# Scores and value products in groups of four, with a lag of four half steps, in the latent attention of an eight-core layer

## What is computed

```
q = xn @ Wq
latent = (xn @ Wk + xn @ Wv) @ W_down_kv          # [S, 256]
k_rec, v_rec = latent @ W_up_k, latent @ W_up_v    # 16 heads of 64
scores = (q_h @ k_h.T) * scale
scores = scores * exp(-1e-4 * |i - j|)             # decay over all pairs i, j
attn = softmax(scores)
out = (attn @ v_h) @ Wo
```

## Time and profile before

| | us |
|---|---|
| median of 5 runs | 14,242.7 |
| lowest and highest of them | 14,153.4 and 14,560.6 |
| the profiled execution | 14,151.7 |
| its span, slowest core | 14,150.2 |
| spans of the 8 cores | 14,133.8 to 14,150.2 |

### The profile page before, as it was taken

The page is one execution under the profiler, slowest core; times in us unless marked ns, Lnnn a source line. Parts: engine busy times, 40 slices in busy tenths (PEclk is TensorE's granted clock), DMA queues, the critical chain, the costliest instruction groups (busy, mean ns, idle before and its releaser), DMA issues. The chain is left out here.

```text
span 14150.2 us, 124711 instructions; the slowest of 8 cores (14133.8 to 14150.2 us)
## 1 busy us (share of the span) xinstructions
PE 12668.3 (90%) x47470; PEld 4550.2 (32%) x48256; DVE 2484.7 (18%) x3494; ACT 3977.7 (28%) x3948; POOL 140.9 (1%) x165
## 2 busy tenths in 40 slices
PE   1789989989998995899999999997799999999998
PEld 0321111111111111344444444443344444444443
DVE  2211121121112112211111111111211111111111
ACT  4135545545554551111111111111111111111111
POOL 0000000000000000000000000000000000000000
PEclk9965555555555556999999999998899999999999
DMA  2000000000000003222222222222322222222222
GB/s 61 33 2 6 5 11 5 5 11 5 5 6 10 6 5 127 54 36 36 42 36 40 38 36 36 36 36 70 73 36 36 36 36 36 39 40 38 41 36 48
DMA packets 201402, 459.02 MB, mean 32 GB/s; under 512 B 12025, under 2 KB 17145, under 8 KB 200066
## 3 DMA queue, kind: packets, MB, share of 16 engines
q0 software_dynamic: 157184, 320.38, 13.3%
q1 hardware_dynamic: 43650, 130.61, 2.8%
HBM read 708.15 MB, written 50.59 MB: 54 GB/s over the span
## 5 line engine op out<-in xcount | busy, mean ns | idle before, releaser
L987 PE MATMUL yp<-wd_sb,a1s 128*128 128x512 bf16 x18060 | 3980.7, 379 | 215.8 <-ACT a1s L1006 196.6
L971 PE MATMUL h1p<-xnTh,wu_sb 128*128 128x512 bf16 x18066 | 3986.5, 379 | 66.9 <-DMA wu_sb<-wut 47.8
L1006 ACT ACTIVATE a1s<-h1p,bu_sb 128x1024 bf16<-128x1024 f32 x1152 | 1282.3, 1113 | 6827.0 <-PE h1p L971 6827.0
L987 PEld LDWEIGHTS yp<-wd_sb,a1s 128*128 128x128 bf16 x18432 | 1793.4, 98 | 2403.2 <-issue 262.2
L971 PEld LDWEIGHTS h1p<-xnTh,wu_sb 128*128 128x128 bf16 x18432 | 1804.4, 98 | 2227.4 <-issue 55.9
L1030 DVE SCALAR_TENSOR_TENSOR comb<-yp,wgt,comb 128x1024 f32<-128x1024 f32 x1024 | 1314.5, 1284 | 5998.0 <-PE yp L987 5998.0
L707 ACT ACTIVATE expT<-scp,consts 128x1024 bf16<-128x1024 f32 x1792 | 1982.4, 1113 | 1343.3 <-PE scp L626 1340.5
L647 PE MATMUL pvp<-expT,vrec 128*65 128x512 bf16 x3584 | 1897.4, 632 | 179.8 <-ACT expT L707 179.8
L626 PE MATMUL scp<-qstg,krecTP 64*128 64x512 bf16 x2304 | 1164.7, 619 | 8.4 <-DVE qstg L757 8.4
L766 DVE TENSOR_TENSOR sTbB<-scp,decayR 128x512 bf16<-128x512 f32 x512 | 328.5, 686 | 3754.0 <-PE scp L626 3753.9
L626 PE MATMUL scp<-qstg,krecTM 64*128 64x512 bf16 x1792 | 923.8, 617 | 0.0
(11 more groups left out here) (105 smaller groups left out, 2122.2 us busy)
## 6 DMA issues: line engine op xcount, KB each, us to landing
wu_sb<-wut POOLq DMA_DIRECT2D x64, 2048.0 KB, 15.8
wd_sb<-wdt POOLq DMA_DIRECT2D x64, 2048.0 KB, 15.5
xst<-x SPq DMA_DIRECT2D x64, 512.0 KB
bcsb<-rr_dram SPq DMA_DIRECT2D x128, 128.0 KB
attn_sp<-ast SPq DMA_DIRECT2D x32, 512.0 KB
att<-attn_sp SPq DMA_DIRECT2D x32, 512.0 KB
wu_sb<-swut POOLq DMA_DIRECT2D x8, 2048.0 KB, 15.7
wd_sb<-swdt POOLq DMA_DIRECT2D x8, 2048.0 KB, 15.4
```

The costliest lines, as they stand in the source:

```text
L971: last = te.matmul(h1p[(tc * NFT + ft) % 2][:, no:no + nw], wu_sb[:, kc * FCB + ft * 128:kc * FCB + (ft + 1) * 128], xnTh[:, kc * TH + tc ...
L987: last = te.matmul(yp[tt % 2][:, no:no + nw], a1s[:, kc * TC + tti * 128:kc * TC + (tti + 1) * 128], wd_sb[:, kc * D + no:kc * D + no + nw ...
L1006: s_s4.inc(sc.activation(a1s[:, ft * TC:(ft + 1) * TC], h1p[(tc * NFT + ft) % 2][:, :], AF.Gelu, bias=bu_sb[:, (e % 2) * 32 + fc * NFT + f ...
```

## The change

Four things change in the second block of each group, and one in the allocation.

1. TensorE's order. Scores and values are issued in blocks of two half steps: scores of `hk0` and `hk0` + 1 (four matmuls), then the values of two half steps taken from a list `pending` that keeps the last `LAG` = 4 half steps back, also over the end of a job; the list is drained at the end of a group. All waits of a block (one for ScalarE, for the later of the exps that free the score tiles and those that feed the values; for `qstg` at a job's start; for the evacuation) stand at its head.
2. `expT` has six slots instead of three, and the diagonal tiles use the same slots: `sTbB` is gone, and so is `rln` (Ln writes into `rr_sb`, and Exp works in place).
3. ScalarE computes Ln and Exp of job J - 1 (`emit_lnrr`) behind the first `LSL` = 4 exps of job J. The first job of a group has two Identity activations of one element there instead, to keep the count. `exp_done` and `rr_done` give the new counts.
4. VectorE's diagonal products wait for the value matmuls of six half steps before, instead of for the end of the previous job.
5. `scp` and `pvp` are allocated once for all groups, and `krp` and `vrp` are parts of `scp[0]` and `scp[1]`; the first block of a group waits for the counts of the group before.

```diff
-                expT = sb2("expT", [128, 3 * 1024], BF16)
-                sTbB = sb2("sTbB", [128, 2048], BF16)
+                expT = sb2("expT", [128, 6 * 1024], BF16)
...
+                LAG = min(4, NHK)
+                LSL = min(4, NHK)
+                SB = SQ2 * JPG + 2
+
+                def exp_done(J, hk):
+                    gj, pj = divmod(J, JPG)
+                    return gj * SB + SQ2 * pj + hk + 1 + (2 if hk >= LSL else 0)
+
+                def rr_done(J):
+                    gj, pj = divmod(J, JPG)
+                    if pj == JPG - 1:
+                        return (gj + 1) * SB
+                    return gj * SB + SQ2 * (pj + 1) + LSL + 2
...
+                scp = [stps2.enter_context(nc.psum_tensor(f"scp{i}", [128, 1024], F32)) for i in range(3)]
+                pvp = [stps2.enter_context(nc.psum_tensor(f"pvp{i}", [128, 512], F32)) for i in range(2)]
...
+                        krp = [scp[0][:, i * 512:(i + 1) * 512] for i in range(2)]
+                        vrp = [scp[1][:, i * 512:i * 512 + 256] for i in range(2)]
...
-                            for pj in range(JPG):
-                                for hk in range(NHK):
-                                    emit_sc(pj, hk)
-                                    if hk >= 1:
-                                        emit_pv(pj, hk - 1)
-                                emit_pv(pj, NHK - 1)
+                            pending = []
+                            for pj in range(JPG):
+                                J, lam, qc = jinfo(pj)
+                                for b in range(NHK // 2):
+                                    hk0 = 2 * b
+                                    pops = []
+                                    pending.append((J, hk0))
+                                    pending.append((J, hk0 + 1))
+                                    while len(pending) > LAG:
+                                        pops.append(pending.pop(0))
+                                    scw = 0
+                                    lh1 = NHK * J + hk0 + 1
+                                    if lh1 >= 3:
+                                        Jp, hkp = divmod(lh1 - 3, NHK)
+                                        scw = exp_done(Jp, hkp)
+                                    for (Jv, hkv) in pops:
+                                        scw = max(scw, exp_done(Jv, hkv))
+                                    if scw:
+                                        te.wait_ge(s_s2m.sem, scw)
+                                    if hk0 == 0:
+                                        te.wait_ge(s_v2m.sem, vseg(J) + 2)
+                                    for (Jv, hkv) in pops:
+                                        if hkv == 0 and Jv >= 2:
+                                            te.wait_ge(s_v2m.sem, evac_done(Jv - 2))
+                                    emit_sc(pj, hk0)
+                                    emit_sc(pj, hk0 + 1)
+                                    for (Jv, hkv) in pops:
+                                        emit_pv(Jv, hkv)
...
+                            def emit_lnrr(Jm):
+                                sc.wait_ge(s_t2m.sem, trec[(Jm, "pv", NHK - 1)])
+                                sc.wait_ge(s_s2m.sem, s_s2m.n)
+                                if Jm >= 1:
+                                    sc.wait_ge(s_bc.sem, dmarec[("rrst", Jm - 1)])
+                                s_s2m.inc(sc.activation(rr_sb[64:65, :], pvp[Jm % 2][64:65, :],
+                                                        AF.Ln))
+                                sc.wait_ge(s_s2m.sem, s_s2m.n)
+                                s_s2m.inc(sc.activation(rr_sb[64:65, :], rr_sb[64:65, :],
+                                                        AF.Exp, scale=consts[64:65, 3:4]))
...
-                                for hk in range(NHK):
+                                for hk in range(min(LSL, NHK)):
                                     emit_exp(pj, hk)
...
+                                if pj >= 1:
+                                    emit_lnrr(J - 1)
...
+                                for hk in range(min(LSL, NHK), NHK):
+                                    emit_exp(pj, hk)
+                            emit_lnrr(JPG * (g + 1) - 1)
...
-                                    if i0 == 0 and J >= 1:
-                                        ve.wait_ge(s_t2m.sem, trec[(J - 1, "pv", NHK - 1)])
+                                    if lh >= 6:
+                                        Jp, hkp = divmod(lh - 6, NHK)
+                                        ve.wait_ge(s_t2m.sem, trec[(Jp, "pv", hkp)])
```

More of the change, by code:

```diff
@@ L523, in evac_done @@
                     return gj * VB + 7 * (pj + 2)
+                LAG = min(4, NHK)
[9 more added lines that the diff above has]
+                    return gj * SB + SQ2 * (pj + 1) + LSL + 2
+                stps2 = stp2.enter_context(ExitStack())
+                scp = [stps2.enter_context(nc.psum_tensor(f"scp{i}", [128, 1024], F32)) for i in range(3)]
+                pvp = [stps2.enter_context(nc.psum_tensor(f"pvp{i}", [128, 512], F32)) for i in range(2)]
                 for g in range(4):
-                    with ExitStack() as stps, nc.Block() as blk:
-                        krp = [stps.enter_context(nc.psum_tensor(f"krp{g}{i}", [128, 512], F32)) for i in range(2)]
-                        vrp = [stps.enter_context(nc.psum_tensor(f"vrp{g}{i}", [128, 256], F32)) for i in range(2)]
+                    with nc.Block() as blk:
+                        krp = [scp[0][:, i * 512:(i + 1) * 512] for i in range(2)]
+                        vrp = [scp[1][:, i * 512:i * 512 + 256] for i in range(2)]
                         T0p, V0p = s_t2p.n, s_v2p.n
@@ L575, in _ @@
                                         krecTP[:, mt * S + nn * 512:mt * S + (nn + 1) * 512],
-                                        krp[gi % 2][:, :],
+                                        krp[gi % 2],
                                         rowP[:, nn * 512:(nn + 1) * 512]))
@@ L591, in _ @@
                             assert s_v2p.n == V0p + 1 + 2 * NKR + NT
-                    with ExitStack() as stps, nc.Block() as blk:
-                        scp = [stps.enter_context(nc.psum_tensor(f"scp{g}{i}", [128, 1024], F32)) for i in range(3)]
-                        pvp = [stps.enter_context(nc.psum_tensor(f"pvp{g}{i}", [128, 512], F32)) for i in range(2)]
+                    with nc.Block() as blk:
                         v2p_done = s_v2p.n
@@ L630, in emit_sc, with emit_pv @@
                                         start=True, stop=True))
[L632 to L639, removed]
+                            def emit_pv(pvJ, hk):
+                                pj2 = pvJ - JPG * g
+                                lam, qc = divmod(pj2, NQC)
+                                lh = NHK * pvJ + hk
+                                u6 = lh % 6
                                 c = None
@@ new lines, in _ @@
+                            if g == 3 or True:
+                                scw = 0
+                                for (Jv, hkv) in pending:
+                                    scw = max(scw, exp_done(Jv, hkv))
+                                te.wait_ge(s_s2m.sem, scw)
+                                for (Jv, hkv) in pending:
+                                    if hkv == 0 and Jv >= 2:
+                                        te.wait_ge(s_v2m.sem, evac_done(Jv - 2))
+                                    emit_pv(Jv, hkv)
+                                pending = []
```

59 lines of the change are left out of this document (26 added, 33 removed).

## The result

The changed kernel took 13,748 us (median of 6 executions, 13,649 to 15,248); the kernel before, now with 10 executions, 14,251 (14,150 to 15,723). The ratio is 0.966, 95% interval 0.961 to 0.971: faster by 3.4%, 500 us. Forecast were 13,690 us, and 13,648 for an execution like the profiled one.

What follows compares the result with a forecast made beforehand. TensorE at 1.2 GHz was taken to bound the attention; four parts, each 126 us shorter (945 against 1071), take 504 from 14,152, giving 13,648, and about half of 91 added gives 13,690 us; range 13,450 to 14,010.

Steps and rivals of the forecast that it cites:

- Fewer changes of shape: TensorE in the attention: a block of four scores and four values takes 3.66 us against 3.92 for two half steps.
- the sum: Attention part: 7.36 + 254 x 3.66 + 3.9 + 1.1 + 3.0 = 945 us against 1071.
- The open term: Four value matmuls in a row: added cost between nothing and 0.13 us a block, 133 us in all; taken as nothing.
- The waits: Values waiting for an exp in an attention part: 69.9 us now, under 10 us after the change.
- Diagonal blocks: One in each of 128 jobs: first exp hidden by 0.1 us; upper bound 141 us if heads wait for the second.
- The row sums: Ln and Exp on ScalarE: exp 4 runs from 9.0 to 10.1, next head due at 11.0; nothing on the path.
- The last job of a head: At qc = 7 VectorE finishes qstg late; the next job's head waits 1.3 us, three times a part, 3.9 us.
- Fill and drain: Ends of a part: second block at 4.82 us, third at 7.36; at the end eight values take 3.0 us.
- the 91 us: Profiled execution lay 91 us under the median of the runs shown; about half was added, giving 13,690 us.
- B: Rival, chance 0.15: values expose a load (133 us), diagonal heads wait (141 us), or both, 13,922 us.
- C: Rival, chance 0.14: the clock rises in the attention parts and ScalarE becomes the bound; 12,370 us if throughout.
- D: Rival, chance 0.09: not faster, block heads wait for late exps; 14,467 us at 0.8 us lost a block.

Runs made afterwards that it cites:

- lag_single: Changed kernel with its blocks split into single half steps (two scores, then two values of four half steps back): part 1009 us, spans 13,894 to 13,916 us.
- scores_tall: Changed kernel with only the score matmuls over 128 rows, half of the query tile zeros: part 620 us, spans 12,343 to 12,361 us.
- lag_two: Changed kernel with LAG = 2 instead of 4: part 973 us, spans 13,750 to 13,766 us.
- sums_early: Changed kernel with LSL = 2, Ln and Exp of the row sums behind two exps instead of four: part 1040 us, spans 14,013 to 14,023 us.
- tall_single: lag_single with only the score matmuls over 128 rows, values left at 128*65: part 591 us, ratio 0.862 to the kernel before.

## Why the prediction was right

*The bound.* TensorE at 0.50 sets the pace of the attention, in both kernels. From a part's last value matmul to the next part's first score it is 70 us in both; only the stretch behind the attention differed in the two profiled executions, by some 20 us, and none of the changed lines lies there.

*Fewer changes of shape.* 0.26 us a block: 3.66 measured on the mean of the plain blocks, as in the sum; lag_single shows it alone, 64 us a part. The open term, four values in a row, was taken at its lower bound and is there (1.92 us). The rule of the Trainium skill cited against it ("TensorE: Matmul & The Clock Gate", Part 3) would have given 133 us more; the trace disagrees for values as it did for scores. What costs is the change between matmuls of 64 and of 128 rows, as scores_tall shows by removing it at the same clock. That it exposes a load fits the trace of the change: within four, a weight load starts 0.43 us ahead of its matmul, beside the matmul before; behind a change it starts with its matmul, 0.56 after the last one of the other kind:

```profile
3008.48 0.19 PEld L653 LDWEIGHTS pvp<-expT,vrec 128*65 128x65 bf16 x2 [0.84 <-issue]
```

*The waits.* Removing them was priced at 68 us a part and brought 62 in lag_single, whose own late query tiles (4.6 us a part) and fill take the rest. Diagonal blocks, on the timeline around one (core 4):

```profile
3028.66 1.89 PE L638 MATMUL scp<-qstg,krecTP 64*128 64x512 bf16 x4
3028.94 0.59 ACT L755 ACTIVATE rr_sb<-pvp 1x512 f32<-1x512 f32 x1 [0.64 <-PE pvp L653]
...
3030.36 2.12 ACT L746 ACTIVATE expT<-scp,consts 128x1024 bf16<-128x1024 f32 x2
...
3032.33 1.89 PE L638 MATMUL scp<-qstg,krecTP 64*128 64x512 bf16 x4
...
3033.11 2.48 DVE L820 TENSOR_TENSOR expT<-scp,decayR 128x512 bf16<-128x512 f32 x4 [26.52 <-PE scp L638]
...
3034.49 2.34 ACT L738 ACTIVATE expT<-expT,consts 128x1024 bf16<-128x1024 bf16 x2 [2.02 <-DVE expT L820]
...
3036.00 1.89 PE L638 MATMUL scp<-qstg,krecTM 64*128 64x512 bf16 x4
```

The products start 0.78 after the scores, the exp 2.16, and the next head goes 3.67 after the last one: hidden by the 0.1 us that the sum had. The row sums too: the job starts at 3021.33, Ln at 7.6 and exp 4 at 9.0 into it, as worked out.

*The last job of a head.*

```profile
2148.26 1.89 PE L638 MATMUL scp<-qstg,krecTP 64*128 64x512 bf16 x4
...
2152.49 0.42 DVE L808 TENSOR_TENSOR qstg<-qT,rowP 64x512 bf16<-64x512 bf16 x1
...
2153.06 1.86 PE L638 MATMUL scp<-qstg,krecTP 64*128 64x512 bf16 x4 [1.06 <-DVE qstg L808]
```

The next job's head is 4.80 us behind, not 3.67: 1.1 us of stall where the sum had 1.3.

*Fill and drain.*

```profile
1917.34 1.86 PE L638 MATMUL scp<-qstg,krecTP 64*128 64x512 bf16 x4 [2.01 <-DVE qstg L808]
...
1922.05 1.86 PE L638 MATMUL scp<-qstg,krecTM 64*128 64x512 bf16 x4 [2.85 <-ACT expT L738]
...
1924.57 1.86 PE L638 MATMUL scp<-qstg,krecTM 64*128 64x512 bf16 x4 [0.66 <-ACT expT L746]
```

```profile
2859.67 3.19 PE L653 MATMUL pvp<-expT,vrec 128*65 128x512 bf16 x8 [0.92 <-ACT expT L738]
...
2868.86 0.68 DVE L796 TENSOR_TENSOR pvst<-pvp,bcsb 64x512 bf16<-64x512 f32 x1 [9.99 <-DMA bcsb<-rr_dram]
...
2880.23 1.86 PE L563 MATMUL scp<-latT,wupk_b 128*128 128x512 bf16 x4 [17.37 <-PEq L612]
```

The second block starts at 4.71 (4.82 in the sum), the third at 7.23 (7.36); eight values take 3.19; the broadcast needs 5.1 us (the Exp of the row sums starts at 2863.75) and the barrier and spill keep their 17. Fill, late heads and drain come out about 1 us a part under the sum; a few short waits that it did not have (0.22 and 0.18 the longest) and plain blocks of 3.662 us give that back. That the lowest execution, 13,649, lies within 1 us of the 13,648 is therefore luck in part; that the part comes out within a few us is not.

*What did not hold.* ScalarE was to stay at 611 us a part; it reads 590, because two exps in a row overlap by 0.1 us (2.12 for two). It was never the bound, so nothing follows; lag_single, where the exps stand singly, reads 611. The added half of the 91 us between profiled execution and median was a guess; the median came 100 us above the lowest.

*The rivals.* B's two prices did not come. Its 141 us for diagonal heads is, by lag_two, 111. C was given 0.14 and did not happen; its premise, that the shapes hold the clock, was right but too wide: the 64 rows of the scores had to go, the 65 columns of the values could stay. Its price, 12,370 us, was met within 30 us once the shape was changed. D's mechanism (the head held by late exps) exists, and sums_early shows it at 3.0 us a job, but in this change ScalarE is never that late.

## What to carry to other kernels

Where matmuls over 64 and over 128 rows alternate, count what a change costs from start to start and issue each kind in runs; and when a lag removes the waits, check where the short instructions between (here the row sums) stand in the stream of the engine that feeds. Before tuning the order of a stage that sits at half clock, try the same work with all 128 rows, zeros included: here that edit was worth 1300 us where the order was worth 500, and it made part of the first tuning unnecessary.

## What the runs showed of the hardware

A score matmul over 128 rows, half of them zeros, with 512 columns streamed, raised the granted clock of the whole attention from 0.50 to 0.98; a value matmul over 128 columns instead of 65 did not raise it at all. I had expected that both shapes would have to be whole, or neither matter. The edit takes away two things at once, the 64 rows and the change between 64 and 128 rows in every block; no run has 64-row matmuls without that change, so which of the two held the clock stays open.

At the full level the clock held although TensorE had pauses: in tall_single it is busy 504 of 592 us and reads 0.99, in the old order with whole shapes it is busy 557 of 764 us and reads 0.93, so there the clock fell back at times. How the level is decided was not tried further.
